# A query projection taken from the raw, transposed input with centred weights, in a fused attention, FFN and expert kernel

## The reference, cut to what matters

```python
x = x + L0_xattn(layernorm(x), ctx, ctx, mask, ...)
x = x + L0_ffn(layernorm(x), weight, bias)        # both sides rounded to a 6-bit grid in blocks of 32
x = x + L1_xattn(layernorm(x), ctx, W, b)
x = x + L1_ffn(layernorm(x), Wg, bg, w1, ..., b3) # 16 experts, each on its 128 best rows

def layernorm(x): return (x - mean(x)) / sqrt(var(x) + 1e-5)
# in L0_xattn:
q = relu(layernorm(x) @ Wq + bias_q)              # Wq is 512 x 512
scores = relu(q @ k.T) / sqrt(512) + mask
out = relu(scores @ v)
```

## Time and profile before

| | us |
|---|---|
| runs of the kernel | 745.37, 745.30, 744.03; median 745.3 |
| span of the profiled execution | 743.2 |
| median less that span | 2.1 |
| PE busy | 716.2 (96% of the span) |
| DVE, ACT and POOL busy | 521.6, 401.9 and 420.4 |

### The profile page before, as it was taken

The page is one execution under the profiler, slowest core; times in us unless marked ns, Lnnn a source line. Parts: engine busy times, 40 slices in busy tenths (PEclk is TensorE's granted clock), DMA queues, the critical chain, the costliest instruction groups (busy, mean ns, idle before and its releaser), DMA issues.

```text
span 743.2 us, 12766 instructions
## 1 busy us (share of the span) xinstructions
PE 716.2 (96%) x4513; PEld 624.9 (84%) x4513; DVE 521.6 (70%) x978; ACT 401.9 (54%) x680; POOL 420.4 (57%) x621
## 2 busy tenths in 40 slices
PE   6999999999999999999999799999999999999994
PEld 5765888888888888888888778798999899899894
DVE  5786789889888888876896697464663565463561
ACT  5755444444544545868668334364664656464641
POOL 2825788888888887786788622503521443340132
PEclk9999999999999999999999899999999999999998
DMA  9610121221222213111117898696796698895534
GB/s 317 256 30 15 43 86 62 88 86 58 88 79 82 71 58 108 52 60 44 49 45 264 322 396 279 149 391 186 222 370 185 185 330 293 289 266 167 142 86 58
DMA packets 61671, 118.04 MB, mean 159 GB/s; under 512 B 6056, under 2 KB 7464, under 8 KB 61608
## 3 DMA queue, kind: packets, MB, share of 16 engines
q1 hardware_dynamic: 54312, 100.44, 38.7%
q0 software_dynamic: 7296, 16.78, 10.3%
HBM read 91.76 MB, written 25.21 MB: 157 GB/s over the span
## 4 chain that ended last, share of the span: by engine, by line
PE 84%; issue 6%; DMA 4%; DVE 3%; ACT 2%; POOL 1%; POOLq 0%; SPq 0%; DVEq 0%; ACTq 0%
PE bank L354 39%; PE banks L354 9%; PE bank L361 6%; PE bank L994 6%; PE banks L861 4%; PE banks L867 4%; DMA out<-y,ids 3%; PE banks L871 2%; PE banks L994 2%; PE banks L872 2%; PE banks L1423 1%; PE banks L1028 1%; PE bank L1318 1%; PE bank L1041 1%; DMA out<-x 1%
## 5 line engine op out<-in xcount | busy, mean ns | idle before, releaser
L2844 POOL DMA_INDIRECT out<-y,ids x24 | 46.1, 1922 | 157.4 <-DVE y L2555 155.5
L1973 DVE TENSOR_TENSOR w_l<-w_raw,w_h 128x2048 fp32r<-128x2048 f32 x35 | 80.1, 2291 | 63.2 <-ACT w_h L1496 49.4
L1961 DVE BATCH_NORM_STATS2 bn<-x 128x6 f32<-128x512 f32 x113 | 77.7, 688 | 8.2 <-DMA x<-x 5.4
L1496 ACT ACTIVATE w_h<-w_raw 128x2048 fp32r<-128x2048 f32 x36 | 68.5, 1918 | 7.2 <-DMA w_raw<-w 7.2
L1892 ACT ACTIVATE h<-bank,b 128x512 f32<-128x512 f32 x48 | 33.0, 688 | 62.5 <-PE bank L354 57.8
L1973 DVE TENSOR_TENSOR hT_l<-h,hT_h 128x512 fp32r<-128x512 f32 x48 | 33.0, 689 | 39.8 <-ACT hT_h L1898 37.7
L354 PE MATMUL bank<-tokT_h,w_h 128*128 128x256 f32 x188 | 55.1, 293 | 0.0
L2607 POOL TENSOR_SCALAR rstd<-mean_var 128x1 f32<-128x1 f32 x108 | 25.7, 238 | 50.9 <-DVE mean_var L1966 42.6
L354 PE MATMUL bank<-tokT_h,w_l 128*128 128x256 f32 x188 | 53.2, 283 | 0.0
L354 PE MATMUL bank<-tokT_l,w_h 128*128 128x256 f32 x188 | 53.2, 283 | 0.0
L354 PE MATMUL bank<-wf_h,xdT_h 128*128 128x512 f32 x128 | 52.6, 411 | 0.0
(11 more groups left out here) (419 smaller groups left out, 2380.1 us busy)
## 6 DMA issues: line engine op xcount, KB each, us to landing
w_raw<-w SPq DMA_DIRECT2D x36, 1024.0 KB
early_w<-w SPq DMA_DIRECT2D x24, 1024.0 KB, 10.0
x<-x SPq DMA_DIRECT2D x32, 256.0 KB, 2.7
out<-x SPq DMA_DIRECT2D x32, 256.0 KB, 2.0
xn<-xn SPq DMA_DIRECT2D x32, 256.0 KB
mask<-mask_t SPq DMA_DIRECT2D x8, 256.0 KB, 3.4
slot_all<-slots SPq DMA_DIRECT2D x4, 512.0 KB, 7.8
stage<-wk SPq DMA_DIRECT2D x1, 1024.0 KB, 7.7
```

Of the source, the lines that this page charges most:

```text
L1496: act.activation(dst, src, ACT.Copy).then_inc(sem, 1)
L1961: dve.bn_stats(bn6[which][:, j % 2, :], src[:, :]).then_inc(sem_bn[which], 1)
L1973: dve.tensor_tensor(dst, src, hi_part, ALU.subtract).then_inc(sem, 1)
L2844: pool.indirect_dma_start(out=out_rows, out_offset=bass.IndirectOffsetOnAxis(ap=ids[:, r:r + 1], axis=0), in_=y[e % 2][b][:, :], in_offset ...
```

## The change

The host gives a second copy of x, turned around (`x_t`). SP loads it a group at a time, 1 MB each, straight into the place of the low part. The high and low parts are now made from that, and the centred weights take away the mean. The product is multiplied by the row's reciprocal deviation afterwards.

* Gone: `norm1`, `t1`, `hi1` and `lo1` (32 each, `t1` with four transposes), `rstd1` per tile, and `warm_up`.
* New on PE: `query_weight_means` (four matmuls, once) and `first_rows` (four transposes, once, for group 0).
* New on ACT: `xt_hi`, two copies of 128x1024 for a group, at k 0 and 1 modulo 4. `q_relu` reads the scaled product from SBUF, makes qT_h before q, and stands behind `hi2`.
* New on POOL: `rstd1` for a whole group (two steps on 128x4, at k 1 modulo 4) and three quarters of the low part (`xt_lo`, 128x512 each, at k 0, 1 and 2 modulo 4), both behind `q_lo`.
* New on DVE: `scaled` for each unit (q = product times rb, in front of the relu), the last quarter of the low part (`xt_lo`, at k 2 modulo 4; for groups 0 and 1 all of it), and at the start the centring of the weights.
* New on SP: `load_xt`, `store_r1` (the group's 512 reciprocal deviations to DRAM) and `load_rb` (the same back, spread over all partitions).

```diff
+        def load_xt(g):
+            if g >= 2:
+                sp.wait_ge(sm.p_q, GRP * (g - 1))
+            sp.dma_start(xt_raw[g % 2][:, :, :], chunked(io.x_t)[:, :, g * GT:(g + 1) * GT])\
+                .then_inc(sem_xt[g % 2], 16)
+        def store_r1(g):
+            sp.wait_ge(sm.g_r1, g + 1)
+            sp.dma_start(io.r1[g * GT:(g + 1) * GT].rearrange("(t p) -> p t", p=P), r1[:, g % 3, :],
+        def load_rb(g):
+            sp.wait_ge(sm.r1_out, 16 * g)
+            sp.wait_ge(sm.d_z, GRP * g)
+            sp.dma_start(rb[:, :], rows_on_all(io.r1[g * GT:(g + 1) * GT], GT)).then_inc(sm.rb_in, 16)
...
         load_x(8)
         load_x(9)
         load_mask(0)
+        load_xt(1)
...
             if n >= 2:
-                pe.wait_ge(sm.a_q, n - 1)
+                pe.wait_ge(sm.d_z, n - 1)
...
-            if valid(k + 9):
-                t1(k + 9)
...
         def q_relu(g, c, n):
-            act.wait_ge(sm.p_q, n + 1)
-            if n >= 2:
-                act.wait_ge(sm.g_qlo, n - 1)
-            act.activation(q32[n % 2][:, :], ps_q[n % 2][:, :], ACT.Relu, bias=bq[:, c:c + 1])
+            act.wait_ge(sm.d_z, n + 1)
             act.wait_ge(sm.p_s, g)
-            act.activation(q_h[:, c, :], ps_q[n % 2][:, :], ACT.Relu, bias=bq[:, c:c + 1]).then_inc(sm.a_q, 1)
+            act.activation(q_h[:, c, :], q32[n % 2][:, :], ACT.Relu, bias=bq[:, c:c + 1])
+            act.activation(q32[n % 2][:, :], q32[n % 2][:, :], ACT.Relu, bias=bq[:, c:c + 1]).then_inc(sm.a_q, 1)
...
         q_relu(*q_of(0))
-        hi1(4)
-        norm1(5)
+        xt_hi(1, 0)
         q_relu(*q_of(1))
-        hi1(5)
-        norm1(6)
+        xt_hi(1, 1)
         q_relu(*q_of(2))
-        hi1(6)
-        norm1(7)
+        setup("wsum")
         q_relu(*q_of(3))
...
+        def scaled(g, c, n):
+            dve.wait_ge(sm.p_q, n + 1)
+            if g == 0:
+                dve.wait_ge(sm.a_set, A["rb0"])
+            else:
+                dve.wait_ge(sm.rb_in, 16 * g)
+            if n >= 2:
+                dve.wait_ge(sm.g_qlo, n - 1)
+            dve.tensor_tensor(q32[n % 2][:, :], ps_q[n % 2][:, :], rb[:, :], ALU.mult).then_inc(sm.d_z, 1)
...
         stats1(5)
         setup("wf scales")
+        scaled(*q_of(1))
...
+            if q_units(k):
+                scaled(*q_units(k)[0])
+            if k % GRP == 2 and 2 <= (k + 6) // GRP < G:
+                xt_lo((k + 6) // GRP)
...
-            if valid(k + 10):
-                rstd1(k + 10)
             if k == 1:
                 q_lo(*q_of(4))
             if not drain(k):
                 for unit in q_units(k):
                     q_lo(*unit)
+            if valid(k + 10) and (k + 11) % GRP == 0:
+                rstd1((k + 10) // GRP)
+            if pool_piece(k) is not None:
+                xt_lo(*pool_piece(k))
```

More of the change, by code:

```diff
@@ L137, in build @@
     bn6 = [place(f"bn{i}", [P, 2, 6]) for i in range(4)]
-    rstd = [place(f"rstd{i}", [P, slots[i], 3]) for i in range(4)]
+    rstd = [None] + [place(f"rstd{i}", [P, slots[i], 3]) for i in range(1, 4)]
+    r1 = place("rstd1_cols", [P, 3, GRP])
     amax = place("amax", [P, NB])
@@ L169, in build @@
     xT1 = [[place(f"xT1_{i}{n}", [P, C, GT], F32R) for n in "hl"] for i in range(2)]
+    xt_raw = [place(f"xT1_{i}raw", [P, C, GT], at=at_xt1 + (2 * i + 1) * 8 * 1024) for i in range(2)]
     at_qt = top[0]
@@ L634, in _ @@
                 load_x(k + XR)
+            if loaded_group(k) is not None:
+                load_xt(loaded_group(k))
+            if stored_group(k) is not None:
+                store_r1(stored_group(k))
             g = k // GRP
@@ L1031, in early_outputs, with query_weight_means, first_rows @@
                 last.then_inc(sm.p_ev, 1)
+        def query_weight_means():
+            for d in range(C):
+                if d % 2 == 0:
+                    pe.wait_ge(sm.c_wq0 if d == 0 else sm.c_wq1, 16)
+                if d == 0:
+                    pe.wait_ge(sm.g_set, GS["mean"])
+                last = pe.matmul(ps_tb[:, :], mean_w[:, :], stage[0][:, d, :], start=(d == 0), stop=(d == C - 1))
+            last.then_inc(sm.p_set, 1)
+        def first_rows():
+            pe.wait_ge(sm.c_ident, 16)
+            pe.wait_ge(sm.g_r1, 1)
+            for t in range(GRP):
+                last = pe.transpose(ps_ta[:, t * P:(t + 1) * P], r1[:, 0, t:t + 1].to_broadcast([P, P]), ident[:, :])
+            last.then_inc(sm.p_set, 1)
         def keys():
@@ L1758, in _ @@
                 setup("crow")
-            j = k + 9
-            if valid(j) and k >= 1:
-                hi1(j)
+            if halves_of_group(k) is not None:
+                xt_hi(*halves_of_group(k))
             if valid(k - 3) and not drain(k):
@@ L2004, in setup @@
                     .then_inc(sm.d_set, 1)
+            if what in ("wqc0", "wqc1"):
+                half = slice(0, 2) if what == "wqc0" else slice(2, 4)
+                dve.wait_ge(sm.p_set, T["wqm"])
+                lo(sm.d_set, stage[0][:, half, :], stage[0][:, half, :],
+                   ps_tb[:, :].unsqueeze(1).to_broadcast([P, 2, D]))
             if what in ("wq0", "wq1"):
@@ L2064, in s_lo_first @@
             dve.tensor_tensor(s_l[:, :], s32[:, :], s_h[:, :], ALU.subtract).then_inc(sm.s_lo, 2)
+        setup("wqc0")
+        setup("wqc1")
+        setup("wq0")
+        setup("wq1")
+        xt_lo(0)
         stats1(0)
@@ L2097, in _ @@
         setup("wf0")
-        lo1(8)
         def logit_parts(g):
@@ L2306, in _ @@
                 setup("va1")
+                scaled(*q_of(4))
             if valid(k - 2) and k - 2 != N - 1:
                 third_low(k - 2)
-            j = k + 9
-            if valid(j) and k >= 3:
-                lo1(j)
             if k == 1:
```

200 lines of the change are left out of this document (83 added, 117 removed).

## The result

The changed kernel takes 778.39 us (median of 776.88 to 780.45, 4 runs) against 745.04: a ratio of 1.0448, 95% interval 1.0429 to 1.0467. The forecast was 750.4, with a range of 741.5 to 755.5. The direction was right; the loss is more than six times the forecast's. The profiled execution has a span of 777.1 us, 33.9 more than before.

A forecast was written before the change was run, and what follows sets the result against it. PE was taken to bound the kernel before, with POOL's path taking back what PE saves in the loop. Span 743.2 + 2.5 (head) + 0.1 (loop) + 2.5 (late) = 748.3; median 750.4, range 741.5 to 755.5 us.

The forecast's parts named there:

- its estimate: Head: xt(1), last in a queue of about 10 MB, was taken to land at 29.7 us.
- the +2.1 of the forecast: Iteration 24: PE's count waits for ACT's probe steps, until 338.8 us instead of 336.67.
- so it is done by T + 0.8 if DVE is free: Loop, DVE: with T the start of t2, `scaled` ends by T + 0.8, before the second relu needs it.
- the 1.01 us: Loop, before the change: POOL has xd ready 1.01 us before t2 uses it, counted as room for new work.
- about nothing, and 0.7 us each time that DVE comes late: Loop, ACT: cost of hi2 ahead of the relus and of `scaled` together; q_lo starts at T + 2.45 against T + 2.44.
- PE's 23.30 stands for these two: Loop, iterations 2 and 3 modulo 4: PE alone sets their two steps, 23.30 us together, against 24.16 before.
- The head's +2.5: Start of the kernel: scores start 3.1 us later, `scaled(4)` adds 0.7, PE saves 1.3; bounds -1 and +4.
- The late iterations' +2.5: Late iterations: +2.1 at iteration 24's count and +0.4 from its neighbours; bounds 0 and +3.5 us.
- the loop's term: Iterations 3 to 20, 4.5 groups: +0.1 us, a group taking 45.32 us against 45.30; -7 to +7 at the ends.
- C: Rival, cold head: PE at 1.2 GHz from the first chunk through four chunks and the values; +8, 758 us; chance 0.07.
- A: Rival, loop: POOL does not bind, PE keeps its 1.72 us a group; 742.6 us; chance 0.26.

The follow-up runs named there:

- e11: Kernel before the change, with one transpose instead of four in t1 from tile 12 on: 742.81 us, ratio 0.9967.
- e9: Changed kernel with e3's POOL order, e4's quarter on DVE, `scaled` ahead of statistics (iterations 0, 1 modulo 4) and of the first residual (24): 761.21 us, ratio 1.0217.
- e6: Changed kernel with the multiplication by the reciprocal deviation left out everywhere; the relus read the product from PSUM: 763.18 us, ratio 1.0252.
- e4: Changed kernel with the low part's quarter of iterations 1 modulo 4 made by DVE instead of POOL: 775.55 us, ratio 1.0433.
- e1: Changed kernel with eight unused products on PE in front of t2 in iterations 6, 10, 14, 18 and 22: 779.95 us, ratio 1.0466.
- e3: Changed kernel with POOL's low parts of units 2 and 3 ahead of the first two dequantised weight rows: 774.08 us, ratio 1.0402.
- e12: Changed kernel with e3's POOL order and 14 unused products on PE before the scores of group 0: 773.34 us, ratio 1.0374.
- e10: Changed kernel without the low part of x (from group 2 on) and without the multiplication by the reciprocal deviation: 747.63 us, ratio 1.0037.
- e2: Changed kernel with `scaled` ahead of the statistics of tile k+10 on DVE in every iteration: 779.4 us, ratio 1.0467.
- e5: Changed kernel with the low part of x not made from group 2 on, the high part used in its place: 762.49 us, ratio 1.0243.
- e8: Changed kernel with only the group's rstd1 on POOL moved to iterations 2 modulo 4, behind xt_lo: 820.9 us, ratio 1.1046.

## Why the prediction was wrong, point by point

**What held.** PE bounds the kernel before (e11). xt_lo, rstd1 and the run that ends with xd have the durations that were taken for them. xt(1) landed 0.7 us from its estimate. In iteration 24 `scaled` stands behind the first residual, and the probe's count waits for ACT.

```profile
367.61 0.27 PE L970 MATMUL bank<-cut_spread,cut_same_row_r 128*128 128x8 f32 x1 [1.92 <-ACT cut_spread L1625]
```

That is the +2.1 of the forecast: at 2.4 GHz the step grows by 2.3 (12.48 against 10.16), and e9, which moves `scaled` there, gets 1.4 of it back. In the changed kernel's trace the clock adds 1.5.

**The step that failed in the loop** is "so it is done by T + 0.8 if DVE is free". The offsets of DVE and ACT from T had been read in a loop in which PE sets T, with xd ready 1.0 us before it. Where POOL sets T, that 1.0 us is gone, T comes that much sooner after DVE's quantisation, and the statistics behind it reach past T. DVE's quantisation began 3.21 us before T (160.44) in the kernel before, and 2.27 before T (177.12) after the change (first fence before, second after).

```profile
157.23 0.69 DVE L2156 TENSOR_TENSOR q<-xc,xrq 128x512 fp8e4<-128x512 f32 x1
```

```profile
174.85 0.69 DVE L2189 TENSOR_TENSOR q<-xc,xrq 128x512 fp8e4<-128x512 f32 x1
```

So `scaled` began at T + 1.28, and q_lo at T + 3.43: 0.98 late, which is what the step from 9 has too much (12.64 against 11.66). In iteration 8 q_lo is 0.47 late, and the step 0.44 too long. The prediction used the 1.01 us as slack for POOL's new work, and at the same time read DVE's place from a loop that still had it. The same step closed with "about nothing, and 0.7 us each time that DVE comes late"; DVE came late each time. It costs 1.4 us a group. With `scaled` out (e6), the steps from 8 and 9 come within 0.1 us of the forecast; with it earlier (e9) q_lo starts sooner and the step from 9 falls by 0.9 beyond e4's.

**The second failure** is "PE's 23.30 stands for these two". In iterations 2 and 3 modulo 4 it is not PE: DVE is busy for 22.81 of 25.19 us there, with `scaled` and its quarter of the low part where lo1 alone had been. Its addition of the mask to the group's scores began 11.77 us behind t2 of iteration 10 in the kernel before (170.99) and took 0.67; now it begins 12.70 behind it and takes 1.25, as its row in the last section shows.

```profile
182.76 0.67 DVE L2055 TENSOR_TENSOR s<-s,mask 128x512 f32<-128x512 f32 x1
```

That is 1.5 of the 1.9 us that the two steps have too much. Even with PE at 2.4 GHz (e1) the two take 25.14, 1.8 more than forecast. POOL alone was followed through the loop; DVE, with 11 us to spare in 90, was not.

**The head's +2.5 was mis-sized**: +8.6 at the first t2, +12.7 at that of iteration 3. The sum followed ACT from the landing of xt(1) to the relus of unit 3 and then put q_lo directly behind; POOL's own order, with 4.28 us of dequantised rows in between, was left out (2 to 4 us by e3). 6.7 us of the head go with `scaled` (e6), up to 4.4 of them by the clock, to which the sum gave nothing. With both sorts of work gone, iteration 3 starts at 98.41, still 4.4 us late (93.97 before): this rest is not resolved into parts. It may lie in the late xt(1), behind which PE and ACT still wait, but no run here moved that load.

**The late iterations' +2.5 was mis-sized too**: +7.4. Iteration 24 has 3.8 of it, 1.5 by the clock. Iteration 21 has 1.8: it is 1 modulo 4 and has the same rstd1 and quarter on POOL as 9, but the loop's term ended at 20 and the late one began at 24. The last 1.8 us are spread over the others and were not followed up.

**The rivals.** None held the time. C had the right sign, but not the place: from the first chunk through the fourth PE ran at 2.4 GHz (a clock of 1.00 over 20 to 40 us). The clock falls to 1.2 GHz later (0.83 over 40 to 60 us, 0.57 over 190 to 194). By the rule of the Trainium skill ("TensorE: Matmul & The Clock Gate", "HAM oscillation — how this bites in real kernels") work that follows a wait for data starts at the slow clock, so that such waits are paid twice. The trace agrees that the level falls behind waits, as behind the 2.36 us in front of 189.76, but not behind each: behind the 2.37 us in front of 286.88 it stayed at 1.00. The price differs too: nothing in iterations 10 and 11 (e1), some 1.5 us in the scores of group 0 (e12), 2.5 in iteration 2 and 1.5 in iteration 24, together some 5.5 of the 33.9 us. A fails on the same `scaled`; even e10, without the work that binds, does not reach 742.6.

The losses then are: some 31 us for the low part and the multiplication on DVE and POOL (e10), the clock's share among them, and 2 to 3 us for the rest of the change, after what PE saved. With all the work still done, 17 us come back by better places (e9). Since even e10 is 0.37% slower than before, no order of these operations that was tried beats the kernel before; that none can is argued from e10, not shown.

## What to carry to other kernels

When work moves off the engine that binds, first ask which loop closes next, and read every offset again relative to that loop: a place "T + 0.5" measured while PE set T says nothing of a loop that POOL or DVE sets, and slack can be spent once. A product that was scaled before by an operation off the path, and is scaled afterwards on the path (product, scale, relu, low part), pays for it in latency in each unit, also where engine time is free. And of each engine that gets work, not only of the one that binds next, the whole period has to be added up in order. After each move, look at what now runs beside it on another engine (0.23 us became 1.20 in e2).

## What the runs showed of the hardware

A store of 512 separate elements of 4 bytes (2 KB) held the load that waited for it 10.2 to 10.8 us, while the 256 KB loads of x land in 3.1 (2.7 in the kernel before). In the window of 190 to 194 us the DMA engines are busy 0.93 of the time at 56 GB/s. The Trainium skill ("DMA: Bandwidth & Descriptors", "Specifications") puts the least size for full rate at 512 bytes; the direction agrees, and the 10 us are from here. No run stored the same 2 KB in larger pieces, so that the small elements are the cause is argued.

The addition of the mask on DVE, with two operands from SBUF, took 0.68 us (median of 8) before and 1.20 after. The rows of the changed kernel show it ending 0.54 us after POOL's addition.

```profile
201.88 1.29 POOL L2749 TENSOR_TENSOR x<-x,ffn_bias 128x512 f32<-128x512 f32 x1
...
202.46 1.25 DVE L2089 TENSOR_TENSOR s<-s,mask 128x512 f32<-128x512 f32 x1
```

It looks as if DVE did not start until POOL was done. No run took POOL's operation away, but e2 moved one: with q_lo of POOL beside them, the two logit operations of DVE took 1.20 and 1.19 us instead of 0.23, in each of iterations 6, 10, 14 and 18. That the two engines slow each other is shown; that DVE stands still meanwhile is argued. The Trainium skill ("GPSIMD Engine Reference", "1. Specifications") names such operations of DVE as those that contend with GpSimd for SBUF, which agrees with the rows.

PE's clock did not always follow the same wait in the same way. In iteration 24 PE waited 1.91 or 1.92 us in front of the probe's count in the changed kernel and in seven runs whose code is the same there; the clock then fell in three traces (the changed kernel, e2 and e5: a step of 13.95 to 13.99 us) and stayed up in five (e1, e3, e4, e8 and e12: 12.48 or 12.49).
